# The second rests of h in a two-layer recurrence: computed by GpSimd in place of VectorE

## What is computed

```python
xW = jnp.einsum('ntd,dh->nth', x, Wx) + b
def step(h_prev, xw_t):
    h_next = jnp.tanh(h_prev @ Wh + xw_t)
    return (h_next, h_next)
_, hs = jax.lax.scan(step, h0, jnp.swapaxes(xW, 0, 1))
...
x = x + _L0_cond_ref(x, cond_1024, L0_cond_Wx, L0_cond_Wh, L0_cond_b)
x = x + _L1_cond_ref(x, cond_1024, L1_cond_Wx, L1_cond_Wh, L1_cond_b)
return x
```

## Time and profile before

| what | value |
|---|---|
| median of 3 runs | 2088.61 us |
| the profiled execution's own time | 2091.38 us |
| its span | 2089.6 us |
| granted TensorE clock, mean | 0.999 |
| PE busy | 2068.7 us (99%) |
| PEld (weight loads) busy | 1793.2 us (86%) |
| VectorE busy | 1722.7 us (82%) |
| ScalarE busy | 1121.9 us (54%) |
| GpSimd busy | 13.2 us (1%), 14 instructions |
| chain that ended last | PE 98%, VectorE 1% |

### The profile page before, as it was taken

How to read it: one execution, slowest core, us unless ns; L and a number is a source line. 1 busy time by engine, 2 the same in 40 slices (tenths; PEclk the granted TensorE clock), 3 DMA queues, 4 the chain that set the end, 5 groups by cost and what they waited for, 6 DMA issues and landing times.

```text
span 2089.6 us, 213893 instructions
## 1 busy us (share of the span) xinstructions
PE 2068.7 (99%) x98460; PEld 1793.2 (86%) x98460; DVE 1722.7 (82%) x10242; ACT 1121.9 (54%) x4612; POOL 13.2 (1%) x14
## 2 busy tenths in 40 slices
PE   7999999999999999999999999999999999999998
PEld 5888888888888888888888888888888888888887
DVE  5888888888888888888888888888888888888887
ACT  3555555555555555555555555555555555555554
POOL 2000000000000000000000000000000000000000
PEclk9999999999999999999999999999999999999999
DMA  3000000000000000000000000000000000000000
GB/s 103 27 23 27 23 27 23 27 23 27 23 27 24 26 24 26 25 25 26 24 26 24 26 24 27 23 27 23 27 23 27 23 27 23 27 23 27 24 26 15
DMA packets 112496, 56.00 MB, mean 27 GB/s; under 512 B 12497, under 2 KB 111073, under 8 KB 112097
## 3 DMA queue, kind: packets, MB, share of 16 engines
q1 hardware_dynamic: 111456, 53.53, 9.0%
q10 hardware_dynamic: 864, 1.18, 0.2%
q0 software_dynamic: 32, 0.02, 0.0%
HBM read 37.90 MB, written 16.78 MB: 26 GB/s over the span
## 4 chain that ended last, share of the span: by engine, by line
PE 98%; DVE 1%; DMA 0%; issue 0%; ACT 0%; SPq 0%; DVEq 0%; ACTq 0%
PE ps_rec L237 43%; PE ps_rec L256 34%; PE ps_xw L216 21%; DMA wh<-wh_in 0%; DVE zt L419 0%; DVE z L425 0%; ACT h L346 0%; DVE h L433 0%; DVE x_mid L459 0%; SPq L182 0%; SPq L184 0%; SPq L180 0%; ACT ps_rec L341 0%; DVE x_out L469 0%; DVEq L418 0%
## 5 line engine op out<-in xcount | busy, mean ns | idle before, releaser
L237 PE MATMUL ps_rec<-wh,h 128*32 128x128 f32 x32848 | 1254.5, 273 | 11.5 <-ACT h L346 8.4
L256 PE MATMUL ps_rec<-wh_part,h 128*32 128x128 bf16 x49056 | 1062.0, 221 | 5.1 <-issue 2.6
L346 ACT ACTIVATE h<-z 128x32 f32<-128x32 f32 x2048 | 470.3, 230 | 831.6 <-DVE z L425 815.2
L237 PEld LDWEIGHTS ps_rec<-wh,h 128*32 128x32 f32 x32848 | 825.2, 109 | 89.8 <-ACT h L346 13.8
L433 DVE TENSOR_TENSOR h<-h 128x16 f32<-128x16 f32 x4088 | 632.4, 155 | 303.9 <-ACT h L346 302.9
L256 PEld LDWEIGHTS ps_rec<-wh_part,h 128*32 128x32 bf16 x49056 | 707.5, 96 | 198.6 <-issue 5.8
L341 ACT ACTIVATE ps_rec<-ps_xw,mask 128x128 f32<-128x128 f32 x2048 | 670.4, 327 | 119.9 <-PE ps_xw L216 95.1
L419 DVE STREAM_TRANSPOSE zt<-ps_rec 128x128 f32<-128x128 f32 x2048 | 639.9, 312 | 18.2 <-PE ps_rec L256 13.6
L425 DVE TENSOR_REDUCE z<-zt 128x32 f32<-128x96 f32 x2048 | 544.7, 266 | 1.5 <-DVE zt L419 0.9
L216 PE MATMUL ps_xw<-wx,x_pe 128*32 128x128 f32 x8232 | 403.7, 273 | 0.0
L216 PE MATMUL ps_xw<-wx,x_mid 128*32 128x128 f32 x8192 | 400.7, 273 | 0.0
(11 more groups left out here) (18 smaller groups left out, 10.4 us busy)
## 6 DMA issues: line engine op xcount, KB each, us to landing
x_pe<-x_t SPq DMA_DIRECT2D x256, 64.0 KB, 1.9
x_dve<-x_t SPq DMA_DIRECT2D x256, 64.0 KB, 2.0
out_t<-x_out SPq DMA_DIRECT2D x256, 64.0 KB, 1.5
wh<-wh_in SPq DMA_DIRECT2D x1, 1024.0 KB, 4.8
wx<-wx_in SPq DMA_DIRECT2D x1, 1024.0 KB, 8.0
wx<-wx_in ACTq DMA_DIRECT2D x2, 256.0 KB, 5.2
wx<-wx_in SPq DMA_DIRECT2D x2, 256.0 KB, 4.9
wh<-wh_in SPq DMA_DIRECT2D x2, 256.0 KB, 7.1
```

Source lines behind the costliest of these rows:

```text
L237: mm = pe.matmul(rows(ps_rec[l][n % 2], g), h_step(l, n - 1)[:, k, :], wh[l][:, k, g * P:(g + 1) * P], start=False, stop=k == KC - 1 and n ...
L256: mm = pe.matmul(rows(ps_rec[l][n % 2], g), h_bits(l, n - 1)[:, k, :], wh_part[l][:, i, at:at + P], start=False, stop=k == KB[l] - 1 and i ...
L346: act.activation(h_of(l, n), z[l][n % 2][:, :].rearrange("p (k b) -> p k b", k=KC), ACT.Tanh).then_inc(h_count(l, n)[0], 1)
```

## The change

The second rests leave VectorE and are made by GpSimd, in the order of the steps, layer 0 and layer 1 in turn. Excepted are layer 0's rests of steps under 8 (`early`) and layer 1's rest of the first h, which VectorE still makes, since GpSimd is then at the weights' parts. GpSimd waits for the first rest (`rest_done`) as VectorE did, and counts up the same semaphore for TensorE. The names `full, rest` in GpSimd's part become `full, left`. In the changed kernel the subtraction has line L182, transpose L435, sum L441, `x_mid` L464 and `x_out` L474.

```diff
+        def early(n):
+
+            return is_split(0, n) and n < RING
+
...
+        def rest(eng, l, n, part):
+
+            step, to, of, tiles = h_step(l, n), h_cols(n, part), h_cols(n, part - 1), slice(0, KB[l])
+            return eng.tensor_tensor(step[:, tiles, to], step[:, tiles, of], h_bits(l, n)[:, tiles, of], ALU.subtract)
+
+        def rest_second(eng, l, n):
+            eng.wait_ge(rest_done[l], n + 1 if l else n + 2 - PARTED)
+            rest(eng, l, n, 2).then_inc(split_count(l, n)[0], 1)
...
+            for l, n in ORDER:
+                if is_split(l, n) and not (l == 0 and early(n)):
+                    rest_second(pool, l, n)
...
             def rest_first(l, n):
                 if is_split(l, n):
                     dve.wait_ge(*h_count(l, n))
-                    rest(l, n, 1).then_inc(rest_done[l], 1)
-
-            def rest_second(l, n):
-                if is_split(l, n):
-                    dve.wait_ge(rest_done[l], n + 1 if l else n + 2 - PARTED)
-                    rest(l, n, 2).then_inc(split_count(l, n)[0], 1)
+                    rest(dve, l, n, 1).then_inc(rest_done[l], 1)
...
-                n0, n1, before = number(0, s), number(1, s), number(1, s - 1)
+                n0, n1 = number(0, s), number(1, s)
                 if n0 is not None:
                     turn(0, n0)
-                if before is not None:
-                    rest_second(1, before)
-                if n0 is not None:
                     lower(0, n0)
                     total(0, n0)
                 sums(s)
                 if n0 is not None:
                     rest_first(0, n0)
+                if n0 is not None and early(n0):
+                    rest_second(dve, 0, n0)
                 if n1 is not None:
                     turn(1, n1)
-                if n0 is not None:
-                    rest_second(0, n0)
-                if n1 is not None:
                     lower(1, n1)
                     total(1, n1)
                     rest_first(1, n1)
```

More of the change, by code:

```diff
@@ L407, in _ @@
                     pool.wait_ge(e, DMA)
-                full, rest = wh[l][:, 0:KB[l], :].rearrange("p k d -> p (k d)"), wh_rest[l][:, :]
-                pool.tensor_tensor(rest, full, upper(full), ALU.subtract).then_inc(s_wrest[l], 1)
+                full, left = wh[l][:, 0:KB[l], :].rearrange("p k d -> p (k d)"), wh_rest[l][:, :]
+                pool.tensor_tensor(left, full, upper(full), ALU.subtract).then_inc(s_wrest[l], 1)
                 pool.tensor_copy(wh_part[l][:, 0, :], upper(full)).then_inc(s_wpart[l], 1)
                 pool.wait_ge(s_wrest[l], 1)
-                pool.tensor_copy(wh_part[l][:, 1, :], upper(rest)).then_inc(s_wpart[l], 1)
-                pool.tensor_tensor(wh_part[l][:, 2, :], rest, upper(rest), ALU.subtract).then_inc(s_wpart[l], 1)
+                pool.tensor_copy(wh_part[l][:, 1, :], upper(left)).then_inc(s_wpart[l], 1)
+                pool.tensor_tensor(wh_part[l][:, 2, :], left, upper(left), ALU.subtract).then_inc(s_wpart[l], 1)
+            for l, n in ORDER:
+                if is_split(l, n) and not (l == 0 and early(n)):
+                    rest_second(pool, l, n)
         @block.vector
@@ L428, in total @@
                                   AX.X, ALU.add).then_inc(z_done[l], 1)
[L430 to L434, removed]
             def rest_first(l, n):
@@ L516, in _ @@
             dve.wait_ge(s_hinit, 2)
-            rest(1, -1, 1).then_inc(s_hrest, 1)
+            rest(dve, 1, -1, 1).then_inc(s_hrest, 1)
             dve.wait_ge(s_hrest, 1)
-            rest(1, -1, 2).then_inc(split_count(1, -1)[0], S4)
+            rest(dve, 1, -1, 2).then_inc(split_count(1, -1)[0], S4)
             for s in range(T + LAG + 1):
```

## The result

The changed kernel takes 2093.44 us (median of 18 runs, 2091.83 to 2095.83), the kernel before beside it 2088.69 us (18 runs, 2088.06 to 2089.83). The ratio is 1.0023 with a 95% interval from 1.0017 to 1.0029: slower by 4.8 us, just over what can be told from no change. Forecast were 2079 us and a range from 2069 to 2130: the time lies in the range, on the other side of no change.

The account below looks back on a forecast made before the run. Bound: the wait for the second rest, 1.0018 us a half-slot. At 0.997, 4.8 ns x 2034 = 9.8 us saved, 0.3 lost at the end: 2091.4 - 9.5 = 2081.9 profiled, 2079 median; range 2069 to 2130.

Parts of the forecast that it names:

- PE's floor: PE's own work in a half-slot, the groups of whole, projection and parts: 0.985 to 0.99 us.
- ring A: Loop in the old kernel: transpose, other layer's second rest queued behind it, parts' weight load, next transpose; 0.99 to 1.00 us.
- ring C: New one-layer loop: first rest, GpSimd's second rest, parts, transpose, sum, tanh; once in two half-slots, 0.9965 us a half-slot.
- X: Time from the first rest's end to the second's: 0.285 us before, forecast 0.08 + 0.20 = 0.28 on GpSimd.
- The release: Lag until GpSimd's subtraction starts after the first rest ends: taken as 0.08 us, upper end 0.14.
- break-even: X = 0.29 us, where the change gains nothing; each further ns costs 0.5 ns a half-slot, about 1.0 us in all.
- Ring B: Loop through first rest, transpose, sum, tanh, first rest: would close in about 0.996 us, with 6 ns of slack.
- The shorter sum: VectorE's sum with no subtraction ahead of it was to take 261 ns against 266, 5 ns off.
- The tail: Layer 1's eight steps alone at the end, 1.95 us each: 0.3 us lost with X at 0.28.
- Rival 1: GpSimd is late and its wait replaces the transpose's: slower, 2118 us at a typical X of 0.32; chance 0.36.
- Rival 2: Ring B already binds, so no change: 2088 to 2089 us; chance 0.16.
- Collisions: GpSimd's subtraction locking out VectorE's two-input work: nothing charged, since transpose and sum cover it until X passes 0.44.

Follow-up runs that it names:

- e1_none: Changed kernel with the moved second rests left out, TensorE's parts waiting for the first rest instead: 2077.0 us, ratio 0.9941.
- e3_memset: Changed kernel with a one-element memset on GpSimd between the wait for the first rest and the subtraction: 2133.63 us, ratio 1.0214.
- e2_tile0: Changed kernel with tile 1's second rest left out, GpSimd subtracting 8 elements a partition in place of 16: 2085.95 us, ratio 0.9983.
- e6_ahead: Kernel before plus an unawaited 128 x 16 GpSimd subtraction, released by the first rest alone, in steps under 700: 2115.16 us, ratio 1.0117.
- e5_beside: Kernel before plus a 128 x 16 GpSimd subtraction that nobody waits for, itself waiting for two semaphores: 2089.77 us, ratio 1.0000.

## Why the prediction was wrong

- **What bounds the kernel: right in the main.** The wait for the second rest held the period, against 98% PE in the chain: without the second rest 12 us are gone (e1_none). PE's floor was put at 0.985 to 0.99 and never came to bind. That it was ring A and not ring C which bound before is not shown: with X = 0.285 ring C would close in (1.713 + 0.285) / 2 = 0.999, within 3 ns of the period too.
- **The new ring and its price: right.** Ring C's rest was put at 1.713. The periods give 2.045 - 0.332 = 1.713 in e3_memset and 2.008 - 0.292 = 1.716 in the changed kernel, and a ns in X costs 1 us there.
- **X: mis-sized, and this step turned the sign.** "I take 0.20" for the subtraction, under an upper bound of 0.21 worked out in the same sentence; it measured 0.213. The release was right, 0.08, though it was read from a single landing of a DMA and not from a first rest, so that it fits is partly luck. X is 0.292, not 0.28, over the break-even of 0.29 that I had named. The bound was the better estimate: from (1.89 - 0.213) / (1024 - 16), an element costs 1.66 ns, just the 1.67 of two streams that I had as the lowest slope, so the whole remainder is fixed. I had shaded it down towards a memset's 0.10 without a row for it.
- **Ring B, relieved: mis-sized, and this step made the gain too large.** It was put at 0.996. e2_tile0 has the X of the forecast (0.28), its transposes stand behind the first rest, and ring B takes 0.9992. I had read 6 ns of slack from the shortest transpose, 307 against a median of 313; in e1_none and e2_tile0 a transpose behind the first rest takes 309 by the median, so it was 4. The sum went from 266 to 267 in e2_tile0 and to 264 in e1_none. That e1_none gives 0.9958, my number to a thousandth, is luck in part: 2 to 3 of the 6 ns there come from the shorter sum, which e2_tile0 and the changed kernel do not have. So even with X as forecast the time is 2086 and not 2079.
- **The shorter sum: not there.** It stayed at 266 ns in the changed kernel, so the subtraction ahead of it was not what made it 5 ns longer; why it varies from 264 to 267 between the runs stays open. This and the two rings' closeness leave 1.4 ns of the changed kernel's period unsettled: 1.0025 by a rest of 1.713, 1.005 by 1.718, 1.0039 measured. Its transposes, 306 to 320 with a median of 316, are a mixture of ones behind the first rest (309) and ones that PE releases (317), which would fit two rings that take turns; no run tests this by itself.
- **The sum, redone.** From the forecast's 0.997 to e2_tile0's 0.9992 is 2.2 ns, 4.5 us, for ring B; from there to 1.0039 by X is 4.7 ns, 9.6 us. Together 14 us, from 2079 to 2093. The tail cost 0.35 where 0.3 was put.
- **The rivals.** Rival 1 came true, at its lower edge, by the mechanism given. Rival 2 fell with e1_none, though ring B lay only 3 ns under the old period and not 6. Collisions were rightly put at nothing: they are real (e6_ahead), but the transpose and the sum cover GpSimd's time. The Trainium skill's "GPSIMD Engine Reference", section "Engine selection", puts GpSimd at about twice VectorE's time for two inputs, from which the prediction had an estimate of 0.26 to 0.35 for the subtraction. The trace does not agree for 16 elements: 0.213, 1.2 to 1.6 times VectorE's 0.175 and 0.132.

## What to carry to other kernels

A chain that is nearly all PE does not say that PE is the bound: look for the load that has no lead before its matmul, follow what released it around until it closes, and compute each ring. A small elementwise step moved off a queue gains only what it stood in the queue, less the other engine's lag and fixed cost; here 0.285 against 0.292. Where a bound from rows has a reason, take the bound and not a value shaded towards the hope. The next ring caps the gain. Where it lies within ten ns of the one that is taken away, the shortest duration in a trace says too little of its length: here it took 0.9958 in one run and 0.9992 in another.

## What the runs showed of the hardware

- GpSimd's subtraction of 16 elements takes 213 ns (changed kernel), of 8 elements 201 (e2_tile0), of 1024 elements 1.89 us: for the small ones nearly all is fixed. It starts 0.08 after the end of VectorE's instruction when it carries the wait itself, and 0.15 after it in e5_beside, where it had two waits. A memset of one element ahead of it costs 0.04 (e3_memset).
- A subtraction of VectorE with two inputs that starts after GpSimd's ends 0.03 behind it (e6_ahead). When both start together VectorE's keeps its 0.13 (e5_beside); GpSimd's took 0.23 there and 0.21 elsewhere, but on operands of its own, so the difference is not shown to be VectorE's doing.
- A transpose behind a subtraction of 128 x 16 starts 0.09 after that one's start at the earliest, and takes 309 ns by the median when its input waits, 317 to 318 when PE releases it (e1_none): its duration tells which of the two held it.
